# Two attention layers: a written-out step order, and bias rows on 128 partitions

## The reference

```python
# layer 0
h = ln(x, ln1);  q, k, v = h @ sa_w* + sa_b*;  rope on q and k
x = x + causal_attention(q, k, v) @ sa_wo + sa_bo
h = ln(x, ln2);  q = rope((h @ ca_wq + ca_bq) / 4);  k, v from the context, rope on k
x = x + attention(q, k, v) @ ca_wo + ca_bo
h = ln(x, ln3);  x = x + gelu(h @ fc1_w + fc1_b) @ fc2_w + fc2_b      # 256 -> 1024 -> 256
# layer 1
q from x, k and v from the context (no rope), causal mask, 16 heads
a = ln(attention + x, ln4);  out = gelu(a @ W1.T + b1) @ W2.T + b2 + a
```

## Time and profile before

| | us |
|---|---|
| median of 3 runs | 1073.44 |
| lowest, highest | 1072.57, 1082.06 |
| the profiled execution | 1076.32 |
| span of its trace, first to last instruction | 1074.5 |
| PE busy in the span | 918.9 |
| DVE busy in the span | 582.3 |
| ACT busy in the span | 420.0 |

### The profile page before, as it was taken

The page is one execution under the profiler, slowest core; times in us unless marked ns, Lnnn a source line. Parts: engine busy times, 40 slices in busy tenths (PEclk is TensorE's granted clock), DMA queues, the critical chain, the costliest instruction groups (busy, mean ns, idle before and its releaser), DMA issues.

```text
span 1074.5 us, 13782 instructions
## 1 busy us (share of the span) xinstructions
PE 918.9 (86%) x5180; PEld 449.3 (42%) x5180; DVE 582.3 (54%) x1347; ACT 420.0 (39%) x822; POOL 73.8 (7%) x83
## 2 busy tenths in 40 slices
PE   3988766999998998988898859999897898997898
PEld 1433332345443363444455325533234444542355
DVE  5756737774677604597646885675036415325500
ACT  1143421451455616454423512277752333243421
POOL 2101100000000200010000001000000000000210
PEclk9998976899999998998999989999998989998999
DMA  8302352001101100331011110111002001020000
GB/s 284 108 21 58 86 145 59 3 1 30 37 25 31 30 1 21 99 85 36 1 30 35 27 30 1 40 31 32 1 21 59 2 7 53 2 59 3 1 20 20
DMA packets 47013, 43.85 MB, mean 41 GB/s; under 512 B 13510, under 2 KB 44386, under 8 KB 46434
## 3 DMA queue, kind: packets, MB, share of 16 engines
q1 hardware_dynamic: 46948, 42.98, 14.2%
HBM read 13.32 MB, written 2.10 MB: 14 GB/s over the span
## 4 chain that ended last, share of the span: by engine, by line
PE 65%; DVE 17%; ACT 8%; issue 3%; DMA 3%; SPq 2%; POOL 0%; ACTq 0%; DVEq 0%; POOLq 0%
PE ps_o L964 11%; PE ps_exp L852 11%; PE ps_misc L835 11%; PE ps_max L889 7%; DVE mcol L1114 6%; ACT probs L1200 5%; PE ps_exp L922 5%; PE ps_chain L814 4%; PE ps_chain L822 3%; PE ps_exp L927 2%; PE ps_chain L787 2%; PE ps_misc L972 2%; DMA xb<-in_x 2%; DVE swap L1028 2%; PE ps_chain L768 1%
## 5 line engine op out<-in xcount | busy, mean ns | idle before, releaser
L1114 DVE TENSOR_REDUCE mcol<-ps_max 128x3 f32<-128x462 f32 (+5 forms) x496 | 291.2, 626 | 156.7 <-PE ps_max L891 94.5
L1200 ACT ACTIVATE probs<-ps_exp 128x512 f32<-128x512 f32 (+3 forms) x544 | 260.8, 522 | 212.5 <-PE ps_exp L927 80.5
L889 PE MATMUL ps_max<-KA,QA 96*128 96x512 bf16 (+3 forms) x384 | 113.0, 346 | 36.5 <-DVE mcol L1114 24.1
L922 PE MATMUL ps_exp<-QA,KA 98*128 98x512 bf16 (+3 forms) x384 | 115.3, 336 | 26.6 <-ACT probs L1200 19.0
L835 PE MATMUL ps_misc<-hT,w_up 128*128 128x512 f32 x256 | 123.0, 603 | 7.2 <-ACT hid L1191 2.2
L852 PE MATMUL ps_exp<-w_down,hid 128*128 128x256 f32 x512 | 127.7, 386 | 0.0
L1191 ACT ACTIVATE hid<-ps_misc,col 128x512 f32<-128x512 f32 x64 | 44.0, 687 | 193.5 <-PE ps_misc L835 193.5
L852 PEld LDWEIGHTS ps_exp<-w_down,hid 128*128 128x128 f32 x512 | 94.1, 190 | 29.7 <-issue 15.3
L1248 POOL TENSOR_TENSOR part<-rot,part 128x512 bf16<-128x512 f32 (+1 forms) x36 | 41.3, 1148 | 882.4 <-DVE part L1038 882.4
L964 PE MATMUL ps_o<-probs,V 128*17 128x512 f32 (+3 forms) x768 | 82.1, 500 | 3.2 <-ACT probs L1200 2.1
L922 PEld LDWEIGHTS ps_exp<-QA,KA 98*128 98x128 bf16 x384 | 35.8, 98 | 112.2 <-ACT probs L1200 90.4
(11 more groups left out here) (109 smaller groups left out, 983.7 us busy)
## 6 DMA issues: line engine op xcount, KB each, us to landing
QA<-part SPq DMA_DIRECT2D x72, 128.0 KB, 2.4
QC<-part SPq DMA_DIRECT2D x72, 128.0 KB, 2.4
KA<-part SPq DMA_DIRECT2D x48, 128.0 KB, 2.4
xb<-in_x SPq DMA_DIRECT2D x8, 512.0 KB, 4.4
out<-xb SPq DMA_DIRECT2D x4, 512.0 KB, 2.9
KC<-part SPq DMA_DIRECT2D x24, 77.0 KB, 2.2
w_up<-in_fc SPq DMA_DIRECT2D x1, 1024.0 KB, 7.9
w_down<-in_fc SPq DMA_DIRECT2D x1, 1024.0 KB, 8.9
```

Of the source, the lines that this page charges most:

```text
L889: mm = pe.matmul(dst, q, kk, start=True, stop=not causal)
L922: mm = pe.matmul(bank[:, q0:CH], KA[:, g // NT, hh, (g % NT) * P:(g % NT + 1) * P], QA[:, hh, q0:CH], start=True, stop=(r < 0))
L1114: dve.tensor_reduce(dst, src, AX.X, ALU.max).then_inc(s_max_done, 1)
L1200: act.activation(probs[:, n % 2, h, q0:CH], ps_exp[exp_nth[s] % 2][:, q0:CH], ACT.Exp).then_inc(s_exp_done, 1)
```

## The change

**Order.** The cost model, the priorities and the choice by waiting time go. A string of 1697 digits names, step by step, the thread whose next step comes; `merged()` replays it with the same threads and the same rules of `before()` and `ready()`, as yes or no instead of times. The set of steps and what a step does are the same.

**Bias rows.** `ones3` and `bias3` are 128 partitions high. `bias3` is cleared by POOL at the start (a memset of 128 x 896 words, POOL's first instruction, with the new semaphore `s_bclear`); SP waits for it ahead of the three DMAs that fill rows 0 to 2. Every bias matmul contracts over 128 rows, 125 of which are zero. Where two token tiles share a PSUM bank (v, wo, the first down), `add_bias_twice` does both in one matmul of 512 columns that reads the bias row twice; the bias then stands ahead of both tiles' products. A v or wo step has one bias matmul, the first down step two, ctxv still five of 256 columns.

```diff
-COST = {
...
-PRIORITY = (6, 4, 1, 7, 8, 5, 3, 2, 0, 9)
...
+MERGE = (
+    "0000000330009933033333303900339333333434343434433445443344534404540554404644434495334444544544305333"
...
-def order():
+def merged(choices):
...
-    while any(at[i] < len(threads[i]) for i in range(10)):
...
-            key = (max(t - free["pe"] - SLACK[i], 0.0), prio)
...
+    for i in choices:
+        if at[i] >= len(threads[i]):
             return None
...
+        s = threads[i][at[i]]
+        if not ready(i, s):
+            return None
...
-    ORDER = order()
+    ORDER = merged(map(int, MERGE))
...
-        ones3 = sb("ones3", [3, P], BF16)
-        bias3 = sb("bias3", [3, len(BIAS_ROWS), E], BF16)
+        ones3 = sb("ones3", [P, P], BF16)
+        bias3 = sb("bias3", [P, len(BIAS_ROWS), E], BF16)
...
             sp.wait_ge(s_bpart, 3)
+            sp.wait_ge(s_bclear, 1)
...
-                pe.matmul(dst, ones3[0:3, 0:m], bias3[0:3, i, :], start=start, stop=False, skip_group_check=True)
+                pe.matmul(dst, ones3[:, 0:m], bias3[:, i, :], start=start, stop=False, skip_group_check=True)
+
+            def add_bias_twice(bank, name):
+
+                once("bias", s_bmove, 48)
+                once("mask", s_mask, 3)
+                both = bias3[:, BIAS_ROWS.index(name):BIAS_ROWS.index(name) + 1, :].to_broadcast([P, 2, E])
+                pe.matmul(bank[:, :].rearrange("p (i e) -> p i e", i=2), ones3[:, :], both,
+                          start=True, stop=False, skip_group_check=True)
...
+                        add_bias_twice(bank, "sa_bv" if k == "v" else s[1] + "_bo")
                         for i in range(2):
                             dst = bank[:, i * E:(i + 1) * E]
-                            add_bias(dst, "sa_bv" if k == "v" else s[1] + "_bo")
...
-                        if m == 0:
+                        if m == 0 and t % 2 == 0:
 
-                            add_bias(dst, ("fc2_b", "l1_b2")[l], start=(t % 2 == 0))
+                            add_bias_twice(ps_exp[t // 2], ("fc2_b", "l1_b2")[l])
...
+            pool.memset(bias3[:, :, :].rearrange("p a e -> p (a e)").bitcast(I32), 0).then_inc(s_bclear, 1)
             pool.wait_ge(s_cols, 16)
```

More of the change, by code:

```diff
@@ L224, in order @@
     at = [0] * len(threads)
[L225 to L228, removed]
+    out = []
+    done = set()
+    rings = {"proj": [], "q": [], "c": []}
     item = hidden = None
[L231 to L237, removed]
     def last_exp(c, hg):
@@ L337, in ready @@
             old = rings[q][-NROW[q]]
-            if ("exp", *old[1:], groups(*old[1:3])[0], 0) not in fin:
-                return None
-        if k == "evac" and len(evacs) and ("turn", *evacs[-1][1:]) not in fin:
-            return None
[L342 to L353, removed]
-    while any(at[i] < len(threads[i]) for i in range(10)):
-        best = None
-        for i in range(10):
-            if at[i] == len(threads[i]):
-                continue
-            s = threads[i][at[i]]
-            t = ready(i, s)
-            if t is None:
-                continue
-            prio = PRIORITY[i]
-            if i in (SMAX, SEXP) and s[2] in CHUNK_PRIORITY:
-                prio = CHUNK_PRIORITY[s[2]][i - SMAX]
-            key = (max(t - free["pe"] - SLACK[i], 0.0), prio)
-            if best is None or key < best[0]:
-                best = (key, i, s, t)
-        assert best, "no step can stand next"
-        _, i, s, t = best
+            if ("exp", *old[1:], groups(*old[1:3])[0], 0) not in done:
+                return False
@@ L373, in order @@
+        if k == "evac" and len(evacs) and ("turn", *evacs[-1][1:]) not in done:
+            return False
+        return all(w in done for w in before(s))
+    for i in choices:
+        if at[i] >= len(threads[i]):
+            return None
+        s = threads[i][at[i]]
+        if not ready(i, s):
+            return None
         at[i] += 1
         out.append(s)
+        done.add(s)
         k = s[0]
-        width = 1.0
-        if k in ("exp", "pv") and s[1] == "sa":
-            width = 1 - max(s[4] - NT * (s[2] % 2), 0) / NT
@@ L379, in order @@
-        for j, (eng, dt) in enumerate(COST[k]):
-            if k == "proj" and eng == "dve" and s[1] == "qla":
-                dt = dt / 3
-            elif k == "stats" and s[3] == 0:
-                dt = 0.7
-            elif k == "up" and eng == "act" and s[3] == 0:
-                dt += 1.3
-            elif k == "exp" and eng == "act" and gelu:
-                dt += 1.3
-            dt *= width if eng == "pe" else 0.25 + 0.75 * width
-            t = free[eng] = max(free[eng], t) + dt
-            t += LATENCY
-            if j == 1:
-                release[s] = t
```

44 lines of the change are left out of this document (22 added, 22 removed).

## The result

The kernel after takes 981.32 us (median of 4 runs, 978.18 to 982.84); the kernel before, run beside it, 1076.38. The ratio is 0.9109, with a 95% interval of 0.9056 to 0.9162. I had predicted 1031, in a range of 1008 to 1060: the sign was right, the gain more than twice what I said (95 us for 42). The profiled execution took 980.38 us with a span of 978.6, at a mean granted clock of 0.953 (0.951 before).

A forecast was written before the change was run, and what follows sets the result against it. The prediction took the kernel as PE-bound, but not everywhere, with many short waits for DVE and ACT. It took 25 us for the bias rows plus 17 for the order, 42 off the 1073.4 median: 1031 us, range 1008 to 1060.

The forecast's parts named there:

- Part A: Bias matmuls on PE: padding to 128 rows removes 0.30 us gaps, 29 us of PE, 25 reaching the end.
- rival 1: Bias matmuls on PE: the gap stays with 128 rows, so the time is 1046 us; chance 0.12.
- Step B: The new step order: fewer PE waits for DVE and ACT, 28 us in terms, 17 us taken.
- The 60%: Discount on the order's 28 us, since a wait that goes is often followed by the next; leaves 17 us.
- runs of exps and maxes: PE's exps and maxes third or later in a run: fewer waits for ACT and DVE, 13.6 and 8.0 us.
- late and reload: SP's queue: chunk 0's reload ahead of the late weights ends a wait of DVE's addition; 5 us.
- Rival 2: Mixed stretches: DVE's maxima and ACT's exponentials bound, waits move, the order is worth nothing, 1048 us; chance 0.20.
- pv and turn: PE's pv steps close behind their group's last exp, turns close behind their last pv: fewer waits, 5 and 4.5 us.
- My two against it, -6 and -4: Losses in the new order: rows close behind their last max, 6 us; first exps close behind rows, 4 us.
- the hole of the earlier trace: PE's 9.8 us wait for a q placement at 640 us: two pv and a turn in between save 2 us.
- Rival 4: SP's queue becomes the bound, row DMAs held behind placements stop PE; slower, 1133 us if 20 held; chance 0.04.
- Rival 3: Whole kernel: bias and order pay in full and the clock holds, 67 us, giving 1006 us; chance 0.14.

The follow-up runs named there:

- e3: e1 with two bias matmuls of 256 columns again instead of one merged, still on 128 rows; 1055.6 us, ratio 0.979.
- e16: Kernel after with bias heights from 3 to 128 rows across its eight first down steps, run once; a step took 2.66 us with 64 rows, 2.17 with 65.
- e1: Kernel before's order with the whole bias part (128 rows, merged matmuls); 1055.01 us, ratio 0.9789.
- e2: Kernel after's order with the bias matmuls of before (three rows, one per token tile); 1006.98 us, ratio 0.9374.
- e9: Kernel after with runs of exps and maxes as long as in the old list; 1003.16 us, ratio 0.9334.
- e11: Kernel after with the late weight loads moved ahead of the q placement and the reload of chunk 0; 988.6 us, ratio 0.9169.
- e5: e1 with 23 copies out of ps_o (evacs) moved up behind their last pv; 1044.71 us, ratio 0.9722.
- e8: e1 with the late weight loads moved behind the reload of chunk 0; 1052.06 us, ratio 0.9783.
- e10: Kernel after with the copies out of ps_o (evacs) as many exps late as in the old list; 995.79 us, ratio 0.9258.
- e19: e1 with its first 205 steps from the new order with old-style runs, copies and late weights, then the old order; 1040.85 us, ratio 0.9673.
- e13: e5 with only exps and maxes exchanged, up to eight places, shortening runs to 64 and 45; 1065.1 us, ratio 0.9894.
- e6: e1 with neighbouring steps exchanged, up to ten places, until runs of exps and maxes were 44 and 19; 1095.12 us, ratio 1.019.
- e4: e1 with the merged bias matmul on 3 rows instead of 128; 1072.8 us, ratio 0.9958.
- e17: e1 with the new order up to the end of chunk 0's first MLP, then the old order; 1037.8 us, ratio 0.9651.

## Why the prediction was wrong

**Part A was right in its mechanism and close in size.** The gap belongs to the height of the bias, 128 rows behave as 96 do, and all 100 gaps went; rival 1 is false (e3, e16). Bare matmul time fell by 35 us where I had 29. 8.1 of it are in the 16 wo steps and 4.1 in the eight v steps (2.45 to 1.94 us each), 8.8 in the eight first down steps (3.26 to 2.16), together 21. With the 0.10 us that stood ahead of the first bias of each of these 32 steps, and that the table counts under "all others", it is 24 us for 80 gaps: 0.30 each, as priced. The term that was mis-sized is ctxv: its four steps gave 14 us, where I had 20 gaps of 0.30, 6 us, and took one off because a few might stay. Three lines of the kernel before and two of the kernel after, the biases for 26 tokens and the product behind the first in PE's timeline:

```profile
29.45 0.28 PE L741 MATMUL ps_chain<-bias,ones 3*26 3x256 bf16 x1
29.66 1.04 PE L768 MATMUL ps_chain<-w_down,a_ctx 128*26 128x256 f32 x4
30.63 0.28 PE L741 MATMUL ps_chain<-bias,ones 3*26 3x256 bf16 x1
```

```profile
31.16 0.38 PE L713 MATMUL ps_chain<-w_down,a_ctx 128*26 128x256 f32 x1
31.16 0.28 PE L678 MATMUL ps_chain<-bias,ones 128*26 128x256 bf16 x1
```

Before, a 26-token block took 1.18 us and they followed one another; after, a block's bias starts with the product of the one before. The four blocks write other output partitions and now run side by side: a ctxv step took 6.00 us and takes 2.51 where the next step does not wait, less than the 4.85 that its columns would take one after the other (an estimate, 20 times 0.215 and five times 0.11). The Trainium skill's rule that I weighed, that a load would lie open in front of each padded bias (page "TensorE: Matmul & The Clock Gate", "Part 3: Packing small matmuls — row/col tiling"), would give a first down step two open loads; the trace disagrees, 2.15 us is its bare column time.

**The share of A that reaches the end** was 85% by my figure, 25 us. It was 22 in the old order, 63% of the 35 us of bare time (e1), and 26, 73%, in the new (e2 against the kernel after). The product of two errors, 35 instead of 29 and less of it passed on, came out right, which is luck. In the old order 12 us of it came back at the q placements (16.2 to 28.1 in the table) and 8 at the maxes: a faster PE gets to a placement earlier, and the placement, as I read it, comes no earlier (no run shows this by itself).

**Step B, the order, is where it failed: 17 us predicted, 70 measured.** Three faults.
- The 60%. Two of my terms were right before the discount: runs of exps and maxes 13.6 + 8.0 = 21.6 us against 22 (e9), late and reload 5 against 7 (e11). "A wait that goes is often followed by the next one" does not hold for the three edits in the new order: undone singly and together they add up, 43.5 and 45. In the old order two of them, done alone, gave less (10 for the copies, e5; 3 for the late weights, not resolved, e8), so it is no general rule either. Rival 2, built on the same thought, is false: the order is worth 70 us, although its sign, a rising share of DVE in the chain (17% to 20%), came. The discount is the smaller fault: without it I had 28 of the 70.
- A row not read. I wrote of pv that the trace "hardly charges PE's matmuls with this" and looked at the wrong producer, the exponentials. The wait for the copy out of `ps_o` stood in the same view, 14.3 us; the 13.8 that went would have been a term of its own. For the turn I had read the wait for that copy, but counted the steps between it and its last pv. e10 leaves both of my counts as in the new list and brings both waits back, 14.5 us: what matters is where the copy stands on ACT. That my 5 + 4.5 = 9.5 for pv and turn came near this is luck.
- What my list lacks. Of the 70 us (74 with the bias part in both: 1055.0 less 981.3), 45 are runs, copies and late weights. My two against it, -6 and -4, came to 3.5 lost ahead of rows (11.1 to 14.6) and 1.9 gained at first exps (8.6 to 6.7). About 14 more us are made in the first 180 us, by the trace in the waits for maxima (e19); some 15 us have no cause shown. I counted a step's neighbours of its own kind only. What DVE does in between, to which 16 of e13's 20 us belong by its trace, I did not count.

**The terms I placed singly.** The reload is early now: in DVE's timeline after, the addition that waited 11.98 us in the earlier trace rows waits for PE's product instead,

```profile
131.69 0.69 DVE L999 TENSOR_TENSOR xb<-xb,ps_chain 128x512 f32<-128x512 f32 x1 [1.54 <-PE ps_chain L767]
```

and the hole of the earlier trace rows is 3.3 us shorter, where I took 2:

```profile
580.53 0.29 PE L834 MATMUL ps_max<-KA,QA 96*128 96x128 bf16 x1 [6.51 <-DMA QA<-part]
```

The memset started at 0.72 us and took 0.84, inside POOL's first wait, as worked out. Rival 4 is false: of PE's waits for row DMAs (QA and QC from `mrow`) after, the longest is 1.2 us. Rival 3, with both parts undiscounted and 1006 us, was the nearest and still 25 us short.

## What to carry to other kernels

Here a bf16 matmul over 64 rows or fewer cost 0.30 us more among full-height float32 ones; zero rows that brought it to 65 or more cost nothing (and gave 22 to 26 of 1077 us). Do not discount a sum of waits without a row that says why: here waits that were undone in one list came back in full and added up. Read every line of that view that has more than one per cent, and ask for each line whether the releaser was late or only stood behind something. In a list of steps for several engines, count for a moved step what each engine that it uses is doing at its new place: drawing runs apart was worth 22 us in one list (34 exps and 16 maxes, e9) and cost 20 (16 and 3, e13) and 40 (36 and 29, e6) in another.

## What the hardware showed beside this

- A matmul of 3, 32, 33 or 64 rows between full ones costs 0.30 us more than one of 65, 96, 97 or 128: one edge, between 64 and 65 (e16; bf16 biases among float32 products).
- Products of 26 output columns to four different blocks of output partitions overlap by themselves, with full-height operands, and stop doing so when 3-row matmuls stand between them: 6.00 against 2.51 us a step (before and e4 against after and e3).
- A lead of 28 us at a fifth of the program was 17 at its end (e17), one of 15 was kept as 14 (e19).
